# Graph attention: the distance mask added on TensorE by sixteen short products, ScalarE's evictions moved to the end of its step, the message multiply placed ahead of the accumulator's sum

## The reference

```python
def _gat_layer(x, src, dst, W, a_s, a_d, b):
    h = (x @ W).reshape(n, HEADS, C)
    s_src = jnp.einsum('nhc,hc->nh', h, a_s)
    s_dst = jnp.einsum('nhc,hc->nh', h, a_d)
    e = jax.nn.leaky_relu(s_src[src] + s_dst[dst], NEG_SLOPE)
    m = jax.ops.segment_max(e, dst, num_segments=n)
    ex = jnp.exp(e - m[dst])
    denom = jax.ops.segment_sum(ex, dst, num_segments=n)
    alpha = ex / denom[dst]
    msg = h[src] * alpha[:, :, None]
    out = jax.ops.segment_sum(msg, dst, num_segments=n)
    return out.reshape(n, HEADS * C) + b
```

## Time and profile before

| | |
|---|---|
| median of 3 runs | 10,745.32 us (10,745.03 to 10,771.93) |
| the profiled execution | 10,737.16 us, of it 10,735.1 us from the first to the last instruction |
| busy share of the span | PE 61%, PE weight loads 49%, DVE 48%, ACT 27%, POOL 50% |
| mean granted TensorE clock | 0.806 of 2.4 GHz |
| the three group loops | about 7,866 to 8,745, 8,839 to 9,712 and 9,806 to 10,680 us |

### The profile page before, as it was taken

The page is one execution under the profiler, slowest core; times in us unless marked ns, Lnnn a source line. Parts: engine busy times, 40 slices in busy tenths (PEclk is TensorE's granted clock), DMA queues, the critical chain, the costliest instruction groups (busy, mean ns, idle before and its releaser), DMA issues. The chain is left out here.

```text
span 10735.1 us, 146502 instructions
## 1 busy us (share of the span) xinstructions
PE 6510.2 (61%) x33621; PEld 5208.7 (49%) x33805; DVE 5158.1 (48%) x13884; ACT 2937.8 (27%) x7335; POOL 5416.5 (50%) x5498
## 2 busy tenths in 40 slices
PE   0013334434463963786778588687567768786876
PEld 0013333423342853665666466466445545554554
DVE  7002223341113225555555555555657757775777
ACT  0000000000000212332333333333245545554554
POOL 2766666646631122554555455455345535553553
PEclk9996666666665986888888888888788888888887
DMA  3201113343330972334335333433323343343333
GB/s 140 62 11 40 39 47 81 85 68 91 92 50 30 360 257 51 80 80 75 77 81 78 75 80 79 74 80 81 54 73 76 77 66 77 77 77 66 77 77 64
DMA packets 614764, 886.30 MB, mean 83 GB/s; under 512 B 285685, under 2 KB 423161, under 8 KB 613408
## 3 DMA queue, kind: packets, MB, share of 16 engines
q0 software_dynamic: 241344, 609.84, 26.4%
q1 hardware_dynamic: 373344, 275.70, 8.5%
HBM read 757.50 MB, written 134.33 MB: 83 GB/s over the span
## 5 line engine op out<-in xcount | busy, mean ns | idle before, releaser
L1534 POOL DMA_INDIRECT hs<-tab_agnn,rec x1952 | 1918.3, 983 | 1714.2 <-issue 532.9
L1967 POOL DMA_INDIRECT hs<-tab_gat,rec x1464 | 1503.0, 1027 | 1172.2 <-DVE msg L2041 620.1
L1654 PE MATMUL psG<-HN,ohT 128*128 x3904 | 1161.3, 450 | 541.0 <-ACT ohT L1610 522.9
L1654 PEld LDWEIGHTS psG<-HN,ohT 128*128 128x128 f32 x3904 | 837.3, 226 | 703.2 <-issue 577.1
L1999 DVE TENSOR_REDUCE mt<-psL 128x2 f32<-128x1024 f32 x732 | 871.9, 1219 | 473.7 <-remote 242.8
L1679 PE MATMUL psV<-hs,pr 128*128 128x258 f32 x3904 | 995.8, 399 | 14.0 <-DVE acc L1581 12.7
L1596 DVE CUSTOM_DVE_ANT_0 prod<-psG,hs 128x256 f32<-128x256 f32 x1952 | 827.5, 480 | 124.7 <-remote 59.7
L1610 ACT ACTIVATE ohT<-psT 128x512 f32<-128x512 bf16 x488 | 291.3, 597 | 2015.9 <-remote 1003.7
L2132 PE MATMUL psV<-msg,oh 128*128 128x260 f32 x2928 | 830.3, 433 | 12.2 <-issue 10.9
L650 PE MATMUL psT<-ident,oh 128*128 128x128 f32 x488 | 120.2, 393 | 1130.3 <-DVE oh L616 1019.9
L1679 PEld LDWEIGHTS psV<-hs,pr 128*128 128x128 f32 x3904 | 737.1, 200 | 112.5 <-DVE acc L1581 15.3
(11 more groups left out here) (324 smaller groups left out, 12803.0 us busy)
## 6 DMA issues: line engine op xcount, KB each, us to landing
w<-in_L_gnn_w SPq DMA_DIRECT2D x224, 512.0 KB, 5.7
fwd_d<-acc SPq DMA_DIRECT2D x10, 3172.0 KB
fw<-fwd_d SPq DMA_DIRECT2D x122, 260.0 KB
hs<-tab_agnn,rec POOLq DMA_INDIRECT x1952
hs<-tab_gat,rec POOLq DMA_INDIRECT x1464
rec<-rec_d SPq DMA_DIRECT2D x1220, 8.0 KB
b<-in_L_gnn_b SPq DMA_DIRECT2D x113, 128.0 KB, 6.8
x<-xbuf SPq DMA_DIRECT2D x112, 128.0 KB, 6.4
```

The lines of the kernel that those rows point to most:

```text
L1534: nc.gpsimd.indirect_dma_start(out=hs[:, j, g, :], out_offset=None, in_=k.tab_agnn, in_offset=bass.IndirectOffsetOnAxis(ap=rec[:, j, g, 0: ...
L1654: mm = nc.tensor.matmul(psG[:, j1 % 2, g, :], ohT[:, j1 % 2, g, :], pick(HN, b, slice(None)).rearrange("p a c -> p (a c)"), start=True, st ...
L1967: nc.gpsimd.indirect_dma_start(out=hs[:, j, g, :], out_offset=None, in_=k.tab_gat, in_offset=bass.IndirectOffsetOnAxis(ap=rec[:, j, g, 0:1 ...
```

## The change

It has three parts. First, PE no longer adds an evicted, scaled copy of the transposed distances to `psL`. It multiplies the untransposed distances themselves: with `away` of one edge tile as the stationary operand (loaded as weights) and a diagonal matrix `far` of -1e30 as the moving one, the product is the transposed distance times -1e30. For one group that is 4 edge tiles times 4 heads, sixteen products with 128 columns, in place of four with 512. ACT's eviction `neg` and its buffer are gone. Second, the steps of ACT and PE are written in another order, and `away` may be overwritten only after the pairs that now read it. Third, DVE multiplies the messages before it adds to the accumulator.

```diff
+        far = sb("far", [P, P], BF16)
+                c.mark(V.tensor_scalar(far[:, :], k.identb[:, :], -BIG, None, ALU.mult))
...
-                            if add:
-                                dve.wait_ge(q.v, nth(t6) + 1)
-                                dve.wait_ge(s_am, own(t6) + 1)
-                                V.tensor_tensor(acc, acc, psV[:, j6 % 2, 0:W_GAT], ALU.add).then_inc(q.u, 1)
                             if old:
                                 dve.wait_ge(q.e, flow(t) + 1)
                                 V.tensor_tensor(hmsg[:, :, :, 0:C_HEAD], hrow[:, :, :, 0:C_HEAD],
...
+                            if add:
+                                dve.wait_ge(q.v, nth(t6) + 1)
+                                dve.wait_ge(s_am, own(t6) + 1)
+                                V.tensor_tensor(acc, acc, psV[:, j6 % 2, 0:W_GAT], ALU.add).then_inc(q.u, 1)
...
                             if old:
                                 _, j4, t = old
                                 h = j4 % 2
                                 if not (isinstance(t, int) and t < 2):
                                     act.wait_ge(q.v, nth(t - 1))
-                                act.wait_ge(s_away, own(t) + 1)
-                                nc.scalar.activation(flat(oh, h), flat(away, j4), ACT.Relu, bias=1.0, scale=-1.0).then_inc(q.oh, 1)
-                            if old:
                                 act.wait_ge(q.tt, own(t) + 1)
...
+                            if now:
+                                i0, _, t0 = now
+                                act.wait_ge(q.rec[j], use(i0, j) * 16 + 16)
+                                if not (isinstance(t0, int) and t0 < U):
+                                    act.wait_ge(q.b, spread(t0 - U + 1))
+                                    act.wait_ge(q.oh, nth(t0 - U + 1))
...
-                                nc.scalar.activation(flat(ohT, j1 % 3), psT[:, 0, :], ACT.Relu, bias=1.0, scale=-1.0)
-                                nc.scalar.activation(neg[:, h1, :], psT[:, 0, :], ACT.Copy, scale=-BIG).then_inc(q.ev, 1)
+                                nc.scalar.activation(flat(ohT, j1 % 3), psT[:, 0, :], ACT.Relu, bias=1.0, scale=-1.0).then_inc(q.ev, 1)
...
+                            def pair(n):
+                                if not (isinstance(t2, int) and t2 < 1):
+                                    pe.wait_ge(s_lt, pairs(t2 - 1) + (n + 1))
+                                for m in (2 * n, 2 * n + 1):
+                                    nc.tensor.matmul(psL[:, m, :], sel[:, m, :], sT[:, h2, :], start=True, stop=False)
+                                for e in range(G):
+                                    for m in (2 * n, 2 * n + 1):
+                                        mm = nc.tensor.matmul(psL[:, m, e * P:(e + 1) * P], away[:, j2, e, :], far[:, :],
+                                                              start=False, stop=(e == G - 1))
+                                mm.then_inc(q.b, 1)
+                            if mid_:
+                                _, j2, t2 = mid_
+                                h2 = j2 % 2
+                                pe.wait_ge(s_st, own(t2) + 1)
+                                pair(0)
...
-                                for m in (2 * n, 2 * n + 1):
-                                    nc.tensor.matmul(psL[:, m, :], k.identb[:, :], neg[:, h2, :], start=True, stop=False)
-                                    mm = nc.tensor.matmul(psL[:, m, :], sel[:, m, :], sT[:, h2, :], start=False, stop=True)
-                                mm.then_inc(q.b, 1)
```

More of the change, by code:

```diff
@@ L1915, in graph_attention @@
                 ohT = sb("ohT", [P, 3, G, P])
-                neg = sb("neg", [P, 2, G * P], BF16)
                 msg = sb("msg", [P, 2, G, W_GAT])
@@ L2051, in step @@
                             now, last, mid_, old = (lagged(i, j, n) for n in (0, 1, 3, 4))
[L2052 to L2060, removed]
                             if old:
@@ L2081, in step @@
                                 nc.scalar.activation(rs[:, j3, :], df[:, j3 % 2, :], ACT.Exp).then_inc(q.rs, 1)
+                            if now:
[4 more added lines that the diff above has]
+                                    act.wait_ge(q.oh, nth(t0 - U + 1))
+                                for g in range(G):
+                                    ins = nc.scalar.activation(away[:, j, g, :], k.iota[:, :], ACT.Abs, bias=recf[:, j, g, 1:2], scale=-1.0)
+                                ins.then_inc(s_away, 1)
+                            if old:
+                                act.wait_ge(s_away, own(t) + 1)
+                                nc.scalar.activation(flat(oh, h), flat(away, j4), ACT.Relu, bias=1.0, scale=-1.0).then_inc(q.oh, 1)
                             if last:
@@ L2147, in step @@
                                 mm.then_inc(q.q, 1)
+                            if add:
+                                _, j5, t5 = add
+                                h5 = j5 % 2
+                                pe.wait_ge(q.msg3, own(t5) + 1)
+                                pe.wait_ge(q.oh, nth(t5) + 1)
+                                if not (isinstance(t5, int) and t5 < 2):
+                                    pe.wait_ge(q.u, nth(t5 - 1))
+                                for g in range(G):
+                                    mm = nc.tensor.matmul(psV[:, h5, 0:W_GAT], oh[:, h5, g, :], msg[:, h5, g, :],
+                                                          start=(g == 0), stop=(g == G - 1))
+                                mm.then_inc(q.v, 1)
                         pipeline(pe, step, 5, numbers=blocks)
```

20 lines of the change are left out of this document (removed).

## The result

The changed kernel takes **10,902.65 us** (10,892.29 to 10,910.44, 4 runs) against 10,745.17 us (4 runs) for the kernel before beside it: 1.0158 [1.0139, 1.0178], slower by 157 us. I had forecast 10,700 us. The loss is all in the three loops: from the first to the last message multiply of a loop a step takes 7.52, 7.57 and 7.52 us on average, 7.13, 7.08 and 7.07 before, +0.44 us over 366 steps = 161 us.

What follows compares the result with a forecast made beforehand. The loop was taken as a DVE step with PE late in about two steps of three. Terms -95 + 8 + 25 + 20 gave -42 us, forecast 10,700 us; 8-in-10 range 10,490 to 10,880, likeliest case 10,640 to 10,725.

Steps and rivals of the forecast that it cites:

- sixteen short products for four wide ones: PE's mask products: 0.90 against 0.88 us a step at the transposes' pace, +8 us over 366 steps.
- -95: PE's transposes no longer wait for ACT's `neg`: half of 191 us of PE idle time reaches the end, -95 us.
- 25: DVE's multiply, now first, idles about 0.1 us a step for the exponentials: +25 us, two thirds of 37.
- 20: ACT's new order: in late steps the exponentials wait for `psV`, now computed after `psQ`: +20 us.
- The multiply's lost cover: DVE's accumulator sum no longer stands before the multiply, which idles about 0.1 us for the exponentials: +25 us.
- Number 5: PE's short products don't keep the transposes' pace: slower, 11,000 us if weight loads don't hide; chance 10%.
- Number 4: ACT's exponentials at L2060 wait for `psV` behind late `psQ`: slower, 10,770 to 10,920 us; chance 17%.
- L2060 waits for PE: Sign of being wrong: ACT's exponentials at L2060 wait for PE or "remote" instead of DVE's logits.
- the first pair waits for `sT`: Sign of being wrong: PE's first pair waits for ACT's `sT`, forecast to be ready just in time.
- the clock is off 0.87 by 0.04: Sign of being wrong: PE's granted clock differs from 0.87 by more than 0.03 either way.
- a spacing of 0.08 us: Sign of being wrong: PE's short products 0.08 us apart or more, against 0.055 to 0.06 forecast.
- Number 2: PE runs unbroken from `psQ` through the second pair and DVE's waits shrink: about -300 us, 10,450; chance 20%.

Runs made afterwards that it cites:

- x1b_split: Kernel before with only its wide mask products split into four each, copy and waits kept, on a late-results chip: 10,736.59 us against 10,574.98, 1.0153.
- x1_split: Kernel before with only its wide mask products split into four each, on the chip with results on time: 9,156.89 us against 9,152.46, 1.0002.
- c3_after: The changed kernel itself, run again on a late-results chip against the kernel before: 10,737.14 us against 10,574.98, 1.0145.
- e4b_short_only: Changed kernel with all three engine orders put back, short products and missing copy kept, late-results chip: 10,686.99 us against the kernel before's 10,575.60, 1.0091.
- c2_after: The changed kernel itself, run again on another late-results chip against the kernel before: 10,728.39 us against 10,575.60, 1.0142.
- e5: Changed kernel with wide mask products and ACT's copy put back, new orders kept, late-results chip: 10,637.41 us against the kernel before's 10,617.43, 1.0020.
- n4: Changed kernel with group-loop indirect gathers replaced by plain transfers of four blocks of zeros, on-time chip: 9,133.79 us against the kernel before's 9,152.46, 0.9978.
- n3: Kernel before with group-loop indirect gathers replaced by plain transfers of four blocks of zeros, on-time chip: 9,133.77 us against 9,152.46, 0.9980.
- e6: Changed kernel with three message buffers, exponentials waiting for the messages' sum of a step earlier, late-results chip: 10,923.09 us against the kernel before's 10,617.43, 1.0280.
- n2: Changed kernel with group-loop indirect gathers replaced by plain transfers of one zero row, late-results chip: 10,472.49 us against the kernel before's 10,575.60, 0.9892.
- e1: Changed kernel with DVE's sum put back ahead of the message multiply, on-time chip: 9,139.58 us against the kernel before's 9,152.67, 0.9984.
- e2: Changed kernel with ACT computing `away` and `oh` ahead of the exponentials again, on-time chip: 9,152.06 us against the kernel before's 9,152.67, 0.9998.
- e4: Changed kernel with all three engine orders put back, short products and missing copy kept, on-time chip: 9,150.42 us against the kernel before's 9,152.67, 0.9996.
- n1: Kernel before with group-loop indirect gathers replaced by plain transfers of one zero row, late-results chip: 10,472.18 us against 10,575.60, 0.9895.

## Why the prediction was wrong

**The step that failed** is "sixteen short products for four wide ones ... I take +8 us". Its pace was right for an unbroken run: in the changed kernel eight short products start at 9320.27 and the next product at 9320.72, 0.056 us each:

```profile
9320.27 0.61 PE L2108 MATMUL psL<-far,away 128*128 128x128 bf16 x8
...
9320.72 0.22 PE L2123 MATMUL psT<-identb,hs 128*128 128x128 bf16 x1
```

But x1b_split puts the term at 10,736.59 - 10,574.98 = **+162 us** (132 to 192 by the interval of its ratio). I took the pace of one unbroken run of transposes for that of every run. Where results are late, runs of short products are broken: PE rests inside the pairs for 100.7 us in x1b_split, waiting for nothing that the profile shows, and x1_split has none of it. In size these rests are about six tenths of the 162 us; that they all reach the end isn't shown, and what makes PE rest stays open. The Trainium skill (TensorE: Matmul & The Clock Gate, "Back-to-back issue gap") would have given an estimate of +282 us by way of a slower pace of every product. No row shows that pace, and x1_split is at 1.0002, though DVE sets that loop. Its warning pointed the right way for another reason.

**The other terms** were -95 + 25 + 20 = -50 us together, and measured next to nothing:
- *All three together*: c3_after is the changed kernel and x1b_split has the split alone, side by side on one chip: 10,737.14 against 10,736.59 us, so +0.6 us for the missing copy and the three orders, within the noise. With +8 in place of 162 the sum comes to about +9 us: without the failed step I would still have missed, with a gain forecast and none there.
- *The copy alone*: e4b_short_only is x1b_split without the copy (and with the distances as operands): 10,686.99 against 10,736.59, on two chips whose kernels before differ by 0.6 us, so about -50. This isn't the -95 of the forecast, which counted the transposes' wait and so PE's new order too.
- *The orders*: c2_after less e4b_short_only is +41 us; with wide products e5 has +20. These too hold what the transposes' wait gave back, so the forecast's +45 for ACT and DVE can't be set against them. What went wrong with the -95 shows in part in the result: the transposes' wait for the eviction went (38.0 us), the 22.9 us for which nothing shows did not (32.1).
- *The multiply's lost cover* alone can be seen: 9.8 / 114 = 0.09 us in n4 and none in n3, the 0.1 us that I forecast; in the changed kernel on the first chip it is 0.55 us, since the exponentials are late themselves.

**The rivals.** Number 5 (short products) had the right part of the change, at 10%: they keep the transposes' pace but not without breaks. Number 4 (exponentials wait for `psV`) is seen in the profile, 69.7 + 16.7 us at L2060, and 10,903 us lies in its range, 10,770 to 10,920; that is luck, since without that wait e6 is slower, and with old orders the loss is there (x1b_split) or most of it (e4b_short_only). A wait that appears isn't yet the cause. Of my signs of being wrong three came: L2060 waits for PE, the first pair waits for `sT` (44.1 us), and the clock is off 0.87 by 0.04; the one that named the short products, a spacing of 0.08 us, did not. Number 2 (PE's late results freed as a whole) didn't come: the new orders alone, which should have freed them, cost 0.2% (e5).

**What I passed over** was in my own rows: `psQ` ended at 9003.36 and was seen at 9007.39, and 106.9 of DVE's 147.9 us were "remote". I wrote that I couldn't explain it and then worked out every term but the rivals as if PE's results were seen when its rows end.

**Shown and not shown.** Shown: splitting the wide products alone brings 1.5% on a chip where results are late and nothing on the one where they are on time (x1b_split, x1_split); it brings rests of PE inside the pairs along; and in these loops both the late results and nearly all of these rests need indirect gathers (c2 against n2, on one chip). Not shown: what in the chip delays the results and what makes PE rest, whether it is one cause, whether it is the number of products or of weight loads (they rose together here, four to sixteen) or the order within a pair, which changed with the split and wasn't tried alone, and why one chip is free of it. That the loss has to do with late results rests on one chip without them. The changed kernel itself wasn't run there; e1, e2 and e4 stand around it, and n4 without gathers. No version with its gathers beats the kernel before where results are late; on the other chip e1_dve_back does, by 0.16%.

## What to carry to other kernels

Don't price more instructions by the pace of one clean run. Look in the whole stretch for idle time inside runs that wait for nothing, and for "remote" waits; where there are some, splitting a wide product into narrow ones isn't neutral even at the same pace and columns. Before you name a wait as the cause, take it away, and ask whether its total goes with the time. A removed wait is worth what its engine's next wait leaves of it. Measure on more than one chip where gathers run beside PE: here the split costs 0.02% on one and 1.5% on another.

## What the runs showed of the hardware

- Chips differ by far more than the change: the kernel before takes 9,152 us on one, 10,575 to 10,617 us on three others and 10,745 us in the first comparison, 16 to 17% more. Without indirect gathers in the group loops it saves 18.7 us on the first (n3) and 103 us on one of the others (n1), though there bound by its transfers.
- On the slower chips a result of PE can be seen over 6 us after the matmul's recorded end, and the lists of waits name "remote" only at lines of loops that gather indirectly; with plain transfers in the group loops (n1, n2) those loops have none. The Trainium skill (Perfetto Trace Analysis, "Per-engine timelines") says that the recorded end is an estimate and the semaphore waits for PSUM's acknowledgement; the traces agree that the two differ, and show that the size of it depends on the chip and on what GpSimd does.
- On such a chip, beside indirect gathers, PE can rest up to 1.2 us inside a run of short products with nothing to wait for: 100.7 us in 190 places in x1b_split, no place in x1_split, the same program on the other chip.
- The granted clock is lower there: 0.98 in the loop on the chip where results are on time, 0.88 in x1b_split, the same program. In the step at 9,078 us PE was idle for 2.66 us, and behind it the clock was at 1.2 GHz, ahead of it at 2.4.
